# Causal attention of a transformer block: a cell's row sums and the next cell's values issued back to back on TensorE

## The reference

```python
Q = _split_heads(x, H)
K = _split_heads(x @ Wk + bk, H)
V = _split_heads(x @ Wv + bv, H)
scores = jnp.einsum('bhqd,bhkd->bhqk', Q, K) + mask     # mask: causal
attn = jax.nn.softmax(scores, axis=-1)
o = jnp.einsum('bhqk,bhkd->bhqd', attn, V)
o = o.transpose(0, 2, 1, 3).reshape(B, S, -1)
return x + jax.nn.gelu(o, approximate=False) @ Wf + bf
```

## Time and profile before

| | |
|---|---|
| median of 3 runs (lowest, highest) | 1045.89 us (1043.09, 1053.1) |
| profiled execution | 1046.96 us |
| its span, first to last instruction | 1045.2 us |
| mean granted TensorE clock | 0.961 |
| PE, DVE, ACT, POOL busy in the span | 86%, 67%, 49%, 25% |

### The profile page before, as it was taken

How to read it: one execution, slowest core, us unless ns; L and a number is a source line. 1 busy time by engine, 2 the same in 40 slices (tenths; PEclk the granted TensorE clock), 3 DMA queues, 4 the chain that set the end, 5 groups by cost and what they waited for, 6 DMA issues and landing times.

```text
span 1045.2 us, 19972 instructions
## 1 busy us (share of the span) xinstructions
PE 899.0 (86%) x7333; PEld 450.0 (43%) x7353; DVE 700.8 (67%) x1675; ACT 509.6 (49%) x886; POOL 260.3 (25%) x405
## 2 busy tenths in 40 slices
PE   2588988788888786857899989999999999999997
PEld 1354545666676665423434433243432223332225
DVE  7799953467888766458765586765679767677204
ACT  1133333233445331434456545766656675666774
POOL 2556520034555754313240000222000000000000
PEclk9899998898999997888999999999999999999999
DMA  5210000000000041050003200000410000000000
GB/s 179 53 42 1 1 0 1 1 1 1 1 1 2 1 75 17 2 89 15 13 23 67 37 18 15 14 3 14 84 28 12 2 12 5 17 4 12 6 7 12
DMA packets 30935, 23.20 MB, mean 22 GB/s; under 512 B 9609, under 2 KB 27897, under 8 KB 30840
## 3 DMA queue, kind: packets, MB, share of 16 engines
q1 hardware_dynamic: 29928, 21.39, 9.4%
q10 hardware_dynamic: 912, 0.54, 0.2%
HBM read 17.32 MB, written 4.34 MB: 21 GB/s over the span
## 4 chain that ended last, share of the span: by engine, by line
PE 59%; DVE 18%; ACT 7%; issue 6%; POOL 6%; DMA 3%; SPq 1%; ACTq 0%; DVEq 0%; POOLq 0%
PE psum L1717 12%; PE psum L1734 11%; PE psum L1691 7%; PE psum L1656 5%; DVE arena L1325 4%; ACT arena L982 3%; PE psum L1603 3%; PE psum L1572 2%; PE psum L1409 2%; PE psum L1614 2%; PE psum L1450 2%; PE psum L1748 2%; POOL rs L712 2%; DMA arena<-scr_parts 1%; PE psum L1500 1%
## 5 line engine op out<-in xcount | busy, mean ns | idle before, releaser
L1325 DVE TENSOR_REDUCE arena<-psum 128x2 f32<-128x1024 f32 (+2 forms) x320 | 336.2, 1064 | 142.4 <-PE psum L1656 79.0
L982 ACT ACTIVATE arena<-psum 128x1024 f32<-128x1024 f32 (+3 forms) x320 | 284.7, 898 | 158.3 <-PE psum L1691 82.5
L712 POOL TENSOR_TENSOR rs<-ve,mhalf 128x1 f32<-128x1 f32 x128 | 72.7, 576 | 363.4 <-DVE ve L1107 363.1
L1717 PE MATMUL psum<-arena 128*32 128x512 f32 (+3 forms) x1280 | 152.5, 549 | 1.3 <-ACT arena L982 1.3
L1734 PE MATMUL psum<-arena,ones 128*32 128x512 f32 (+3 forms) x1280 | 150.2, 541 | 0.9 <-DVE arena L1352 0.8
L1656 PE MATMUL psum<-arena 48*128 48x512 bf16 (+3 forms) x640 | 111.6, 351 | 30.6 <-DVE arena L1325 10.1
L1691 PE MATMUL psum<-arena 50*128 50x512 bf16 (+3 forms) x640 | 114.2, 357 | 17.1 <-DMA arena<-arena 10.3
L1691 PEld LDWEIGHTS psum<-arena 50*128 50x128 bf16 x640 | 31.1, 93 | 196.6 <-issue 115.4
L818 POOL TENSOR_TENSOR arena<-arena 128x512 f32<-128x512 f32 x15 | 19.1, 1273 | 232.8 <-DMA arena<-scr_sums 232.8
L951 ACT ACTIVATE rh<-psum,fb 128x128 f32<-128x128 f32 x128 | 36.6, 368 | 57.9 <-PE psum L1603 57.9
L1656 PEld LDWEIGHTS psum<-arena 48*128 48x128 bf16 x640 | 35.7, 94 | 57.8 <-DVE arena L1325 19.0
(11 more groups left out here) (187 smaller groups left out, 1490.0 us busy)
## 6 DMA issues: line engine op xcount, KB each, us to landing
arena<-scr_parts SPq DMA_DIRECT2D x96, 64.0 KB
arena<-scr_sums SPq DMA_DIRECT2D x60, 64.0 KB, 2.0
scr_parts<-arena SPq DMA_DIRECT2D x12, 256.0 KB, 2.6
arena<-arena SPq DMA_DIRECT2D x124, 2.0 KB, 1.8
X<-in_L_attn_src_dram SPq DMA_DIRECT2D x4, 256.0 KB, 4.5
out_dram<-X SPq DMA_DIRECT2D x16, 64.0 KB, 1.6
arena<-in_c_zsel_dram SPq DMA_DIRECT2D x1, 512.0 KB, 3.7
arena<-in_L_attn_Wk_dram SPq DMA_DIRECT2D x1, 512.0 KB
```

The costliest lines, as they stand in the source:

```text
L712: v.tensor_tensor(rs[:, u, t:t + 1], ve[:, u, t:t + 1], mhalf[:, :], ALU.pow).then_inc(s_rstd[u], 1)
L982: v.activation(pr[:, u % RING, pp, :, 0:CH - off], both(("scores", n))[0][:, :, off:CH], ACT.Exp).then_inc(s_p, 1)
L1325: v.tensor_reduce(MXP[:, j, 2 * pp:2 * pp + 2, m], both(("max", g, pp, j, m))[0][:, :, 0:hi - lo], AX_X, ALU.max).then_inc(s_mxd, 1)
L1717: last = mm(bank(O_BANK)[VD * h:VD * h + VD, off:CH], V[kb // TPC][:, kb % TPC, GH * (g % GPC) + h, :], pr[:, u % RING, h // 2, h % 2, 0:C ...
```

## The change

Cells are walked in pairs u, u+1 with u even. Where the three cells u-1, u, u+1 are all full and the group is 4 or higher (36 pairs), the twelve parts of the four halves are put in the order of `PATTERN`; elsewhere the order stays. S stands for the scores of a half, M for its maxima, P for its product and what else is due there.

```diff
+PATTERN, PATTERN_FROM = "SMPSMSPPMSMP", 4
...
-            for u in range(max(at) + 1):
+            def half_cell(u, i):
...
+                first = [x for x in here if x[0] == "gelu" and i == 0] + [x for x in slot if x[0] == "row_max"]
+                while scored[0] < min(GP * u + i + 1 + ahead.get(2 * u + i, 0), GP * len(CELLS)):
+                    first.append(("scores", scored[0]))
+                    scored[0] += 1
+                product = []
+                if 0 < u <= len(CELLS):
+                    product.append(("values" if i == 0 else "sums", u - 1))
...
+                product += others[cut * i:cut * (i + 1)] + [x for x in slot if x[0] not in ("row_max", "max")]
+                return {"S": first, "M": [x for x in slot if x[0] == "max"], "P": product}
+
+            scored = [0]
+            for u in range(0, max(at) + 1, 2):
+                halves = [half_cell(u + k // GP, k % GP) for k in range(2 * GP)]
+                plain = u < len(CELLS) - 2 and all(CELLS[n][1] < TPC * (CELLS[n][0] // GPC) for n in (u - 1, u, u + 1))
+                taken = {"S": 0, "M": 0, "P": 0}
+                for kind in PATTERN if plain and CELLS[u][0] >= PATTERN_FROM else "SMP" * (2 * GP):
+                    out += halves[taken[kind]][kind]
+                    taken[kind] += 1
```

More of the change, by code:

```diff
@@ L482, in causal @@
                             put(first + k + (last and k > 3), name, 2 * TILES + t)
-            ahead, scored = {}, 0
+            ahead = {}
             for c in range(CHUNKS - 1):
@@ L488, in causal @@
             out = [x for k in sorted(slots) if k < 0 for x in slots[k]]
-            for u in range(max(at) + 1):
+            def half_cell(u, i):
                 here = at.get(u, [])
                 others = [x for x in here if x[0] != "gelu"]
-                out += [x for x in here if x[0] == "gelu"]
                 cut = (len(others) + 1) // 2
[L494 to L508, removed]
@@ new lines, in half_cell @@
+                slot = slots.get(2 * u + i, [])
+                first = [x for x in here if x[0] == "gelu" and i == 0] + [x for x in slot if x[0] == "row_max"]
[5 more added lines that the diff above has]
+                    product.append(("values" if i == 0 else "sums", u - 1))
+                    g, kb = CELLS[u - 1]
+                    if g + 1 == MGROUPS and kb >= TPC * (CHUNKS - 1):
+                        product.append(("take_tile" if i == 0 else "invert_tile", kb % TPC))
+                    elif kb == TPC * (g // GPC + 1) - 1:
+                        product.append(("take_o" if i == 0 else "take_d", g))
```

## The result

| | median of 16 runs | lowest to highest | profiled execution | its span | granted clock |
|---|---|---|---|---|---|
| before, on the same chip | 1045.85 us | 1040.25 to 1053.1 | 1046.96 (the one of the tables ahead) | 1045.2 | 0.961 |
| after | 1053.53 us | 1050.93 to 1057.39 | 1053.38 | 1051.6 | 0.959 |

The ratio is 1.0067, with a 95% interval of [1.0047, 1.0086]: 5 to 9 us slower. The forecast was 1055, the range 1046 to 1062. A second measurement of the same kernel gave 1.0097 [1.0061, 1.0133].

The account below looks back on a forecast made before the run. It took PE's issue plus its waits as the bound. Some 15 us lost less 5.8 saved gave +9.3 on the 1045.89 us median, forecast 1055 us, range 1046 to 1062.

Parts of the forecast that it names:

- The main step: Each S or M waits for the reader three places before; three now stand without a product: some 15 us lost.
- `d_hidden` behind V(u): Pairs 62, 74, 114, 118, 122: M3 waits 0.7 to 0.8 us for four relus, 0.5 comes back; +1.0 in all.
- The six beside them: Pairs 64, 66, 76, 78, 116, 120 wait a little for `e_v`, `d_add` or a bunched reduction: +0.4 us in all.
- 34 and 42: Two pairs where S2 waits for relus (0.7 us) and M3 for `d_add` (1.65): +1.7 each, +3.4 in all.
- Group 11: Pairs 86, 88, 90, three M in two halves: late reductions or an exponential cost +1.1, +1.4, +0.7 us; together +3.2.
- the 0.16 that a join saves: Joining Q(u-1) and V(u) saves 0.09 us entering and 0.08 leaving, together 0.16 or so a pair; 5.8 over 36 pairs.
- group 15: Five pairs without M: V(u) waits for S1's exponential until 2.92 us, not 2.78; 0.04 saved a pair, 0.2 in all.
- clean pairs: Group 14, five pairs: S2 waits for M0's reduction, 0.75 us lost against 0.8 saved: nothing left.
- the other five: Pairs 18, 26, 50, 104, 106: savings go to copies, a gelu wait, or stay under 0.1 us; about 0.
- Banks come free in time: Rival for all pairs: only the shape switches count, 5.8 us faster, 1040.1 us (1038 to 1043); chance 0.10.
- The old slack takes in half: Rival: PE's 14 us of old waits shrink, absorbing half of the lost 15; 1047.5 to 1051.5 us; chance 0.20.
- The waits grow into one another: Rival: DVE's reductions in groups 8 to 13 still queue at the next pair; +16, 1062 us, half 1058; chance 0.26.

Follow-up runs that it names:

- short reductions: Row-maximum reductions on DVE read only every fourth score: old order 1023.41 us (0.9779 of the kernel before), new order 1025.22 us (0.9780), its second execution 1031.33 us.
- the change again: The changed kernel, nothing altered, measured a second time against the kernel before: 1057.22 us, ratio 1.0097.
- the two halves alone: Against the kernel before: only M2 moved behind V(u), 1.0069, stretch +8.82 us; only S2 moved ahead of Q(u-1), 1.0031, stretch +4.75 us.

## Why the prediction was right, point by point

**The main step held.** Three set-taking steps in a row, without a product between, show the readers' lengths to PE: the short reductions took 8.5 down to 0.6 with the same order of steps. S2 of a clean pair came 2.02 behind S0, forecast 2.03. After a reduction a set was free 0.14 to 0.15 behind its end, as in the earlier trace rows. Behind a wide diagonal S2 of pair 132 came 2.25 behind S0, for 2.43.

**`d_hidden` behind V(u).** M3 waits 0.69 for the relus (above), forecast 0.7 to 0.8; the five pairs +1.25 (+1.03 in the change again), forecast +1.0. The six beside them were put at +0.4 and came to nothing.

**34 and 42.** S2 waits for relus and M3 for `d_add`, the latter 1.30 for 1.65: +3.02 for +3.4. The rows at 34, timeline after, hold the first wait as well:

```profile
595.57 0.39 PE L1701 MATMUL psum<-arena 50*128 50x512 bf16 x2 [0.69 <-ACT rh L961]
```

**Group 11.** All three waits are where they were put (timeline, after): S2 of 86 for the second reduction; in 88 four reductions stand one behind the other, 4.35 us, and an M waits 0.98 for 1.1 forecast; S2 of 90 waits for S1's exponential. +2.74 for +3.2.

```profile
797.92 0.39 PE L1701 MATMUL psum<-arena 50*128 50x512 bf16 x2 [0.74 <-DVE arena L1335]
...
807.12 4.35 DVE L1335 TENSOR_REDUCE arena<-psum 128x2 f32<-128x1024 f32 x4 [1.96 <-PE psum L1666]
...
808.49 0.39 PE L1666 MATMUL psum<-arena 48*128 48x512 bf16 x2 [0.98 <-DVE arena L1335]
...
812.95 0.39 PE L1701 MATMUL psum<-arena 50*128 50x512 bf16 x2 [0.78 <-ACT arena L992]
```

**Mis-sized: the 0.16 that a join saves.** Where nothing waits it is 0.24: pairs of group 14 with short reductions, -0.24 each. The exit was taken at 0.08 from one 256-column sample; for 512 columns product to product is 0.88 to 0.89 against 1.00, so 0.12 at the exit, which was the wide bound's value, 0.09 at the entry, and 0.03 more because V to M2 takes 0.97. Over the 31 pairs outside group 15 that is 2.5 us, and it accounts for most of the differences in the classes that were put too high: clean pairs, the other five, the six beside `d_hidden`. "Nothing left" in group 14 was wrong for that reason. In group 15 V(u) waits some 0.1 for the exponential, forecast 0.14 (Q to V 0.98 rather than 0.89), and a pair saves 0.13 for 0.04.

**Missing: the cells behind the pairs, +2.14.** Behind the last pair of groups 8, 11, 12 and 14 DVE still has the reductions of M2 and M3 in its queue, and what comes next on PE waits for them. Behind 55, 91 and 107 that is mainly the next M (timeline, after: behind V(55), then behind V(91)):

```profile
683.93 0.39 PE L1666 MATMUL psum<-arena 48*128 48x512 bf16 x2 [0.62 <-DVE arena L1335]
...
819.88 0.39 PE L1666 MATMUL psum<-arena 48*128 48x512 bf16 x2 [0.24 <-DVE arena L1335]
```

Behind 139 it is `turn_max`, in which PE turns the row maxima: it waits for `row_max` on DVE, now queued behind the two reductions (timeline behind pair 138, after):

```profile
978.10 2.36 DVE L1335 TENSOR_REDUCE arena<-psum 128x2 f32<-128x1024 f32 x2 [1.22 <-PE psum L1666]
...
980.96 0.17 DVE L1349 TENSOR_TENSOR arena<-arena 128x16 f32<-128x16 f32 x1
981.19 0.60 PE L1684 MATMUL psum<-ident,arena 128*8 128x128 f32 x4 [0.26 <-DVE arena L1349]
```

Before, the same turn stood without a wait, 0.54 behind the start of `row_max`'s last row, where 0.23 lies between them now (timeline, before):

```profile
973.56 0.18 DVE L1339 TENSOR_TENSOR arena<-arena 128x16 f32<-128x16 f32 x1
...
974.10 0.60 PE L1674 MATMUL psum<-ident,arena 128*8 128x128 f32 x4
```

The prediction walked the steps inside each pair and stopped at its last one. That these cells pay for the crowd's reductions is shown: they cost nothing more with short reductions, and nothing with S2 alone moved. The two errors, 2.5 too little saved and 2.1 not counted, nearly cancel. So it was luck that the sum, +9.3, met the stretch's 9.0 (9.6 with the half clock) so closely; by classes it missed by up to 0.7.

**The rivals.** *Banks come free in time*: its -5.8 doesn't appear. Even with short reductions the new order, in all groups but 10, is 0.6 above the old one, since waits for relus and exponentials stay; only in the clean pairs is its condition met there (-0.24 each). With full reductions those pairs gain 0.08 each, and the others lose far more. *The old slack takes in half*: half of M's 9.0 us of waits for exponentials did go (4.7 left), but that was largely in the forecast as 0.5 at seven places. *The waits grow into one another*: the two halves alone would add up to 6.6 and give 9.0 together, so there may be some of it, but by pair these are mostly gains that fail to add up, and they stay under the 3 to 7 of that rival. That one wait stands behind another is shown at `d_add`: 2.6 us of waits taken away brought 1.2.

**Signs named ahead.** Groups 6, 7 and 11 were to be longer by 2 to 3 each: +2.03, +1.74 and +3.27, and without the half clock groups 6 and 7 fall short, at +1.54 and +1.62. Waits of PE for reductions were to go from 5.4 to over 10: 8.6 at M and 1.5 at S, 10.1 (5.4 and 0.8 before). Q to V was to be 0.92: 0.88 to 0.89.

**By the rule on drains** (the Trainium skill, "TensorEngine Tiling (Array Packing)", section Tiling Modes) a change of tiling mode drains TensorE, and one within a mode doesn't. The traces agree: removing two changes of mode saved 0.24 us a clean pair with short reductions, and each half of the change alone, which removes none in group 14, saved nothing there (+0.3 over its five pairs).

**Left open.** The first measurement gives 5 to 9 us, the second 6 to 14; 9.6 lies just outside the first's interval and inside the second's. What the parts ahead of V(0) and behind V(159) do isn't resolved, since single executions scatter there by more than the difference. Whether the half clock at V(40) belongs to the change is open as well: both profiled executions of the changed kernel have it, and none of the other twelve has one there. Why the reciprocal waits 8.8 us for its gather in one execution and nothing in others wasn't followed, nor how much a wait of 4 us from it adds to the scatter of the times.

## What to carry to other kernels

Before you join work that needs no buffer, count how many steps that take a buffer then stand in a row, and set the distance from each to the step k places on (k buffers) against the reader's start, length and wake-up, reader by reader, with what queues ahead of it on its engine. Walk on past the last moved step to the next step that depends on any of the bunched readers. Choose place by place: the new order gained 0.1 to 0.2 us in most calm pairs and cost up to 0.4 where four relus stood in the crowd, and 0.7 to 1.5 where a third reduction or an addition did. So a uniform pattern lost 9 us by the trace, where a chosen one, with the other steps moved out of the crowd, won 4.5.

## What the runs showed of the hardware

- A float32 product run of 512 columns in four column tiles takes 1.00 us to the next bf16 run of another shape and 0.88 to 0.89 to a like run; behind a joined one the exit to M is 0.97. The gain of the join is thus more than the two changes of shape as single gaps show it.
- PE starts 0.14 to 0.15 us behind the end of a reduction or an exponential of 1024 a partition that it waits for (963.34 to 963.48 in pair 134), and 0.05 to 0.06 behind the end of a relu (899.01 to 899.07 in pair 114) or of `d_add` (600.71 to 600.76).
- A reduction from PSUM goes by the elements that it reads, not by the span that it walks: 1024 a partition take 1.224 us, every fourth of them 0.425, as much as a run of 256 takes (0.424).
- In a stretch where the order is fixed, no wait ends on a DMA and the granted clock is the same, distances repeat from one execution to another within 0.01 to 0.02 us, while the whole time scatters by 10 us. A difference of 1 us can thus be read from two single traces, step against step.
- The granted clock can fall inside such a stretch. At 0.50 (1.2 GHz) for 3.4 us it cost 0.6 us at V(40) of the changed kernel, in both of its profiled executions. In the new order with short reductions it fell to 0.50 for 6.8 us while PE stood still for 4.00, and pairs 74 and 76 lost 2.2 us beside that wait. Before a difference is put down to an order, the clock of both stretches is to be compared.
